# One image per half pass: another order of all steps in a fused transformer tower on one core

## The chip, the cores and the metric

The kernel runs on one core of a Trainium2 chip. Time is the device time of one launch in microseconds (us), all 64 images, loading of weights and storing of results included. Engines are named by what they do: TensorE (PE, products; PEld is its loading of weights), VectorE (DVE), ScalarE (ACT), GpSimd (POOL), SyncE (SP, here the one that issues DMAs). Each has a queue of its own and takes it strictly in order; between engines there are only semaphores.

## The reference

For 64 images of 3x224x224:

```python
h = tok(x)                                   # 16x16 patches: layernorm, 768->192, layernorm, class token
h = h + attn(layernorm(h))                   # 12 heads of 64; q and k scaled by their norm over the heads
h = h + ffn(layernorm(h))                    # attention 2: 12 heads of 16, qkv with a gated LoRA delta (8 experts, top 2)

# attn
q, k, v = split(x @ w_qkv.T)                 # 3 x 768
q = q * rsqrt(norm(q, over heads) + eps);  k likewise
out = softmax(q @ k.T / scale[h]) @ v;  return out @ w_out.T + b_out
# ffn
probs = softmax(x @ Wg.T + bg);  combine = top 2 of probs
delta = ((x A + ba) * combine) @ Bm + combine @ bb
qkv = x @ Wqkv.T + bqkv + 2 * delta
return softmax(q @ k.T / 4) @ v @ Wproj.T + bproj
```

197 tokens an image, width 192, all float32.

## The kernel before

The work of one image is cut into named steps. Each step is a piece for several engines: TensorE makes products into banks of PSUM, ScalarE or VectorE read them, later steps use what they wrote. The steps, in the order in which an image passes them:

- X (ScalarE squares of the patches into qk_sq, GpSimd sums them), EMB (embedding product), LA, LB, LC (layernorms on VectorE, GpSimd gives 1/sqrt), T1 (transpose of the hidden state; ScalarE copies it rounded to 16 bit, VectorE the remainder).
- Attention 1: QK.0 to QK.2 (queries and keys; ScalarE squares them into qk_sq and copies them), S (VectorE adds the squares), PS (product that adds pairs; ScalarE makes 1/sqrt of the norm in four passes), N.0 to N.3 (N.0, N.2: VectorE scales; N.1, N.3: ScalarE writes the high half qh or kh, VectorE the low half), V.0 and V.1 (values), SM.0 to SM.5 (scores of two heads each from the high halves; VectorE takes each row's maximum, after SM.5 it negates them), NT (transpose of the maxima; ScalarE copies them to neg_t), ST.0 to ST.5 (exact scores, transposed, minus the maximum; ScalarE takes the exponential into one of four ebufs), PV.0 to PV.2 (four heads each: row sums first, of which ScalarE makes the reciprocal, then the product with the values), M.0 to M.2 (VectorE multiplies with the reciprocal), OP (output projection, and VectorE adds), LD (layernorm), T2 (transpose).
- Attention 2: G and GB (gates), T3, QK2.0, QK2.1, V2, SM2.0 to SM2.2 (four heads each), NT2, ST2.0 to ST2.2, PV2.0 to PV2.2, M2.0 to M2.2, OP2, and the stores.

ORDER (line 51) is the order in which every engine issues its part of the steps, written out by hand. One run through it is a half pass: it begins one new image. A sign ahead of a step says whose: "+" the next image's, none this image's, "-" the previous one's, "=" the one before that. The number behind "@" is the first PSUM bank of the step. `half_pass` (line 62) reads it for the images of either parity; two half passes make one turn of the loop, and there are 32 turns, with half passes ahead of them and behind them in which only a part of the steps has an image. QK, V, SM, ST and PV take two banks, SM2 and ST2 four, all others one.

A step waits on TensorE until its banks have been read by whoever used them last (`users`, `reader`), and for its inputs. The waits are worked out from the order: `Pass.count` and `Pass.previous` find how often a semaphore has been raised when a given step of this or of the turn before is done, `wait` (line 342) emits the wait. So a new order moves the work and the waits and changes no instruction. Buffers that several steps share by turns: qk_sq (X and QK; freed by X's sums and by S), qh, ql, kh, kl (one set; N writes them, SM and ST read them), four ebufs (ST and ST2 in turn), two rinv.

The shapes of the products, as rows x columns of the array: T1, T2, T3, NT, NT2, QK, QK2, PS, EMB, V, V2, OP, OP2 and G use the whole array (98 to 128 rows); SM and ST 64 rows; SM2 and ST2 32 rows; PV and PV2 32 columns.

Of the kernel before, what the change touches and what calls it, by code (L numbers as in the profile page):

```python
# [27 lines left out]
NT = NP + 1  # L28
# [20 lines left out]


ORDER = """
+X T1@4 =QK2.0@1 =QK2.1@0 QK.0@2 =SM2.0@4 QK.1@0 QK.2@2 =SM2.1@4 -ST.3@0 -ST.4@4 -ST.5@2 -PV.1@6 S
-M.1 =SM2.2@0 -PV.2@4 PS@1 =NT2@7 -M.2 N.0 N.1 N.2 +EMB@2 -OP@3 N.3 =ST2.0@4 V.0@0 SM.0@2 =ST2.1@4
-LD =V2@0 SM.1@4 SM.2@2 -T2@6 =PV2.0@7 SM.3@4 =M2.0 =ST2.2@0 =PV2.1@6 SM.4@4 SM.5@0 -G@7 =PV2.2@2
NT@4 V.1@0 ST.0@4 =M2.1 ST.1@6 +LA =M2.2 -GB +LB ST.2@2 =OP2@5 -T3@4 +LC PV.0@6 M.0
"""


# [17 lines left out]
POS = {p: n for n, p in enumerate(SCHED)}  # L76
# [9 lines left out]
def banks(p):  # L86

    return range(BANK[p], BANK[p] + (4 if p[0] in QUAD else 2 if p[0] in WIDE else 1))


def head2(u, j):

    return 2 * j + u if u < 2 else 8 + j
# [60 lines left out]
def vit_tower(nc, x_t, w_emb, ln1, ln1_bias, tok_const, tok_bias, w_qk, w_v, w_out, w_gl, w_qkv2, w_lora_b,  # L154
# [4 lines left out]
    with ctx:  # L159
# [182 lines left out]
        def wait(eng, now, sig, p, earlier=None, by=1):  # L342


            n = now.count(steps[sig[0]], p, earlier)
            if n is not None:
                eng.wait_ge(sig[1], n * by)

        def reader(p, bank=None):

            if p[0] in QUAD and bank is not None and bank < BANK[p] + 2:
                return rd_lo[p[0]], p
            return rd_sig[p[0]], ({"PV": "M", "PV2": "M2"}.get(p[0], p[0]), *p[1:])

        def wait_free(eng, now, order, freed):


            q, earlier = now.previous(order, now.at)
            wait(eng, now, *freed(q), earlier)

        def passes(eng, body):
            body(Pass("start", -1))
# [15 lines left out]
        for j in range(4):  # L378
            loads.append((sel2_raw[32 * j:32 * j + 32], head_rows[64:96, 0:G2]))
            for u in range(2):  # L380
                g, r = divmod(head2(u, j), 4)
# [15 lines left out]
        for part in range(3):  # L397
            r = slice(64 + GPITCH * part, 64 + GPITCH * part + NE + 1)
# [129 lines left out]
        def _(pe):  # L528
# [38 lines left out]
            def body(now):  # L567
                for p in now.steps():
# [12 lines left out]
                            pe.wait_ge(setup_dve, 5)  # L581

                    freed = [(b, *now.previous(users[b], p)) for b in banks(p)]
                    for sig, q, earlier in dict.fromkeys((*reader(q, b), earlier) for b, q, earlier in freed):
                        wait(pe, now, sig, q, earlier)
                    if kind == "EMB":
                        pe.wait_ge(x_loaded[s], (now.image(p) + 1) * 16)
# [38 lines left out]
                    elif kind == "SM":  # L626
                        wait(pe, now, high_N, ("N", s, 3))
                        for t in range(2):
                            for e in range(2):
                                r = slice(64 * e, 64 * e + 64)  # L630
# [3 lines left out]
                    elif kind == "SM2":  # L634
                        wait(pe, now, high_QK2, ("QK2", s, 1))
                        for t in range(2):
                            for j in range(4):
                                r = slice(32 * j, 32 * j + 32)
# [7 lines left out]
                    elif kind == "ST":  # L646
                        wait(pe, now, qkn_ready, ("N", s, 3))
                        wait(pe, now, rd_sig["NT"], ("NT", s, 0))
                        for t in range(2):
# [3 lines left out]
                            for n, (left, right) in enumerate(terms):  # L653
                                for e in range(2):
                                    r = slice(64 * e, 64 * e + 64)
                                    nc.tensor.matmul(ps(p, slice(0, TR), slice(NT * t, NT * t + NT), e),  # L656
                                                     left[r], right[r], start=(n == 0), stop=False)
                            for e in range(2):
                                r = slice(64 * e, 64 * e + 64)
# [3 lines left out]
                    elif kind == "ST2":  # L663
                        wait(pe, now, rd_sig["QK2"], ("QK2", s, 1))
                        wait(pe, now, rd_sig["NT2"], ("NT2", s, 0))
                        for t in range(2):
# [4 lines left out]
                            for n, (left, right) in enumerate(terms):  # L671
                                for j in range(4):
                                    r = slice(32 * j, 32 * j + 32)
# [80 lines left out]
                    mm.then_inc(pe_sig[kind][1], 1)  # L754

            passes(pe, body)

        @block.scalar
        def _(act):
# [11 lines left out]
            def body(now):  # L771
                act.sem_clear(act_chain)
                count[0] = 0
                for p in now.steps():
# [3 lines left out]
                    if kind == "X":  # L778
# [3 lines left out]
                        if not first:  # L782
                            wait_free(act, now, sq_users, squares_used)
                            if now.image(p) == 0:
                                act.wait_ge(setup_dve, 2)
# [11 lines left out]
                    elif kind == "QK":  # L797
                        wait(act, now, pe_sig[kind], p)
                        src = psum[:, b:b + 2, 0:2 * NT]
                        if i == 0:  # L800
                            wait_free(act, now, sq_users, squares_used)
# [43 lines left out]
                    elif kind in ("ST", "ST2"):  # L845
                        wait(act, now, pe_sig[kind], p)
                        for half in range(2 if kind == "ST2" else 1):
                            n = e_order.index((p, half)) % EBUFS
                            wait_free(act, now, e_users[n], exp_used)
                            nc.scalar.activation(  # L850
                                ebuf[n].rearrange("p e a t -> p e (a t)"),
                                psum[0:TR, b + 2 * half:b + 2 * half + 2, 0:2 * NT], ACT.Exp
                            ).then_inc(rd_lo[kind][1] if kind == "ST2" and half == 0 else done, 1)
# [450 lines left out]
```

## Time and profile before

| | us |
|---|---|
| median of the runs (3) | 3115.53 |
| lowest, highest | 3112.74, 3116.41 |
| the profiled execution, its own time | 3115.51 |
| its span in the trace | 3113.7 |
| TensorE busy | 2965.3 (95%) |
| VectorE busy | 2328.8 (75%) |
| ScalarE busy | 1963.5 (63%) |
| GpSimd busy | 591.9 (19%) |

A busy matmul row is not the array at its peak: matmuls overlap, and their ends are modelled. Starts are recorded; so the length of a step on TensorE is read as the distance from its first start to the first start of the next step. The views print a group of like instructions with its start, the time it covers and, in brackets, the idle time before it and what ended it.

### The profile page before, as it was taken

The page shows a single profiled execution, that of the slowest core. Times are in us where ns is not written, and L with a number is a line of the kernel's source. Part 1 is how long each engine was busy: PE and PEld are TensorE (multiplying, and loading weights), DVE is VectorE, ACT ScalarE, POOL GpSimd, SP SyncE. Part 2 cuts the span into 40 slices and gives each one's busy share as a digit, 9 for nine tenths or more (in the row PEclk, how much of TensorE's full clock was granted, in tenths as well). Part 3 has the DMA queues.
Part 4 walks back from the last instruction along what each step waited for, and adds up shares of the span by engine and source line. Part 5 has one row for each costly group of instructions (what it writes and reads, how often), then busy time and mean ns, then how long its engine had stood idle before and what let it go on. Part 6 is the DMA issues. An engine that isn't in the chain of part 4 may idle for free.

```text
span 3113.7 us, 98361 instructions
## 1 busy us (share of the span) xinstructions
PE 2965.3 (95%) x41624; PEld 2430.5 (78%) x41624; DVE 2328.8 (75%) x5441; ACT 1963.5 (63%) x3777; POOL 591.9 (19%) x859
## 2 busy tenths in 40 slices
PE   4899999999999999999999999999999999999996
PEld 4778877877877877877877888778778778778775
DVE  5777777777777777787777777777777777777773
ACT  2566666666666666666666666666666666666663
POOL 2111121121121121121121121121111111111210
PEclk7999999999999999999999999999999999999998
DMA  4000000000000000000000000000000000000000
GB/s 116 9 22 12 22 22 12 21 22 12 21 22 12 22 22 12 22 21 12 22 21 12 22 22 12 22 17 16 22 14 19 22 12 21 22 12 22 14 4 7
DMA packets 28389, 61.28 MB, mean 20 GB/s; under 512 B 4210, under 2 KB 18389, under 8 KB 27958
## 3 DMA queue, kind: packets, MB, share of 16 engines
q1 hardware_dynamic: 27958, 54.98, 6.1%
q8 instruction: 337, 5.52, 0.8%
q14 instruction: 94, 0.77, 0.1%
HBM read 45.29 MB, written 9.68 MB: 18 GB/s over the span
## 4 chain that ended last, share of the span: by engine, by line
PE 59%; DVE 35%; ACT 3%; issue 3%; DMA 0%; SPq 0%; POOL 0%; DVEq 0%; ACTq 0%
PE psum L686 9%; DVE mx L1118 8%; PE psum L695 8%; PE psum L590 8%; PE psum L612 7%; PE psum L622 4%; PE psum L722 4%; PE psum L674 3%; PE psum L656 3%; DVE st L1009 3%; DVE mx L1131 2%; PE psum L725 2%; DVE qk L1210 2%; PE psum L732 2%; DVE late L1227 2%
## 5 line engine op out<-in xcount | busy, mean ns | idle before, releaser
L850 ACT ACTIVATE ebufs<-psum 99x788 f32<-99x788 f32 x768 | 592.0, 823 | 58.1 <-PE psum L674 45.1
L519 POOL TENSOR_TENSOR veps<-mv,eps_ln 99x2 f32<-99x2 f32 x256 | 116.1, 453 | 2274.1 <-DVE mv L1040 1352.3
L1131 DVE TENSOR_REDUCE mx<-psum 99x4 f32<-99x788 f32 x384 | 357.5, 974 | 137.7 <-PE psum L639 137.4
L1118 DVE TENSOR_REDUCE mx<-psum 99x4 f32<-99x788 f32 x384 | 362.9, 974 | 52.1 <-PE psum L631 52.1
L612 PE MATMUL psum<-hn_s,qk_w 128*128 128x197 f16 x3840 | 354.9, 249 | 14.2 <-DVE hn_s L1082 7.2
L612 PEld LDWEIGHTS psum<-hn_s,qk_w 128*128 128x128 f16 x3840 | 323.0, 98 | 34.9 <-DVE qk L1210 19.0
L686 PE MATMUL psum<-ebufs,vx 98*32 98x197 f32 (+1 forms) x6144 | 293.6, 330 | 0.0
L695 PE MATMUL psum<-out_w,qk 128*99 128x192 f32 x1536 | 263.8, 329 | 0.1
L590 PE MATMUL psum<-emb_w,xb 128*99 128x193 f32 x1536 | 263.9, 327 | 0.0
L590 PEld LDWEIGHTS psum<-emb_w,xb 128*99 128x99 f32 x1536 | 249.1, 166 | 1.8 <-issue 1.4
L686 PEld LDWEIGHTS psum<-ebufs,vx 98*32 98x32 f32 (+1 forms) x6144 | 201.2, 110 | 57.5
L695 PEld LDWEIGHTS psum<-out_w,qk 128*99 128x99 f32 x1536 | 245.1, 166 | 0.3 <-issue 0.3
L622 PE MATMUL psum<-v_w,hn_s 128*99 128x384 f16 x1280 | 234.1, 330 | 0.0
L656 PE MATMUL psum<-qh,kh 64*99 64x197 f16 x1536 | 208.5, 255 | 17.5 <-DVE mx L1131 17.0
L1101 DVE TENSOR_TENSOR qk<-qk,ss 128x1182 f32<-128x1182 f32 x64 | 89.0, 1391 | 168.0 <-ACT ss L826 168.0
L802 ACT ACTIVATE qk_sq<-psum 128x788 f32<-128x788 f32 x192 | 158.8, 827 | 70.6 <-PE psum L612 70.6
L656 PE MATMUL psum<-ql,kh 64*99 64x197 f16 x1536 | 202.1, 246 | 0.0
L660 PE MATMUL psum<-neg_t,head_sel 64*99 64x197 f16 x1536 | 201.9, 246 | 0.0
L656 PE MATMUL psum<-qh,kl 64*99 64x197 f16 x1536 | 201.8, 245 | 0.0
L622 PEld LDWEIGHTS psum<-v_w,hn_s 128*99 128x99 f16 x1280 | 155.0, 127 | 47.1
L831 ACT CAST kh<-qk 128x1182 f16<-128x1182 f32 x64 | 75.6, 1181 | 176.4 <-DVE qk L1106 176.4
L1148 DVE TENSOR_TENSOR qk<-psum,rinv 128x394 f32<-128x394 f32 x192 | 108.9, 567 | 102.8 <-ACT rinv L861 62.1
(172 smaller groups left out, 6444.3 us busy)
## 6 DMA issues: line engine op xcount, KB each, us to landing
xb<-x_t SPq DMA_DIRECT2D x64, 591.0 KB, 3.9
out<-h SPq DMA_DIRECT2D x128, 73.5 KB
out<-h SPq DMA_DIRECT2D x64, 0.8 KB
vx<-w_qk SPq DMA_DIRECT2D x2, 384.0 KB, 11.2
qk_sq<-w_emb SPq DMA_DIRECT2D x1, 576.0 KB, 3.7
vx<-w_qk SPq DMA_DIRECT2D x1, 576.0 KB, 8.3
out_w<-w_out SPq DMA_DIRECT2D x8, 72.0 KB
late<-w_lora_b SPq DMA_DIRECT2D x1, 480.0 KB
```

Of the source, the lines that this page charges most:

```text
L590: nc.tensor.matmul(ps(p, slice(0, TR), slice(194 * t, 194 * t + D + 1)), xb[s][:, c, tile_cols(t)], emb_w[:, c, :], start=(c == 0), stop=( ...
L612: mm = nc.tensor.matmul(ps(p, slice(0, 128), slice(at, at + NT), m // 2), qk_w[:, w, f:f + 128], hn_s[s][:, v, c, 0:NT], start=(n == 0), s ...
L622: mm = nc.tensor.matmul(ps(p, slice(0, TR), slice(0, INNER // 2), b), hn_s[s][:, v, c, tile_cols(i)], v_w[:, w, INNER // 2 * b:INNER // 2 ...
L656: nc.tensor.matmul(ps(p, slice(0, TR), slice(NT * t, NT * t + NT), e), left[r], right[r], start=(n == 0), stop=False)
L660: mm = nc.tensor.matmul(ps(p, slice(0, TR), slice(NT * t, NT * t + NT), e), head_sel[r, 2 * i + e, :], neg_t[s][r, 0:NT], start=False, sto ...
L686: mm = nc.tensor.matmul(ps(p, slice(32 * j, 32 * j + 32), slice(NT * (c % 2), NT * (c % 2) + NT), c // 2), left, eb[0:n, j % 2, t, :], sta ...
L695: mm = nc.tensor.matmul(ps(p, slice(0, TR), slice(D * t, D * t + D)), o_t[s][:, m, tile_cols(t)], out_w[:, m, :], start=(m == 0), stop=(m ...
L722: nc.tensor.matmul(o, qkv2_w[:, w, f], hn2_s[s][:, v, c, 0:NT], start=(n == 0), stop=False)
L802: nc.scalar.activation(qk_sq[:, 4 * i:4 * i + 4, :].rearrange("p (b m) t -> p b (m t)", b=2), src, ACT.Square, scale=1 / WS)
L850: nc.scalar.activation(ebuf[n].rearrange("p e a t -> p e (a t)"), psum[0:TR, b + 2 * half:b + 2 * half + 2, 0:2 * NT], ACT.Exp).then_inc(r ...
L1118: nc.vector.tensor_reduce(mx[s][:, :, 2 * i:2 * i + 2].rearrange("p a e -> p e a"), psum[0:TR, b:b + 2, 0:2 * NT].rearrange("p e (a t) -> ...
L1131: nc.vector.tensor_reduce(mx2[s][:, :, at:at + 2].rearrange("p a e -> p e a"), psum[0:TR, b + 2 * half:b + 2 * half + 2, 0:2 * NT].rearran ...
```

## The change

All of ORDER is written anew: the order of the steps, their signs and their banks. Seen from an image, SM.2 to SM.5, NT, ST.0 to ST.2, PV.0 and M.0 come in the half pass after the one in which they came before ("-" instead of none); SM.0 and SM.1 stay in it, at its end. T3 goes from "-" to "=", T1 from none to "+" (from the start of a half pass to the end of the one before). The other steps keep their sign and change places and banks. SM stands in pairs, ST.2 to ST.5 in one run, PV.1 beside PV.2 and PV2.1 beside PV2.2.

The second part lets a wait be worked out where the step that used a bank or a buffer is of the turn before, but the step that frees it of this turn: `release` says "earlier" only where the freeing step is at or behind the user in the order.

```diff
 ORDER = """
-+X T1@4 =QK2.0@1 =QK2.1@0 QK.0@2 =SM2.0@4 QK.1@0 QK.2@2 =SM2.1@4 -ST.3@0 -ST.4@4 -ST.5@2 -PV.1@6 S
--M.1 =SM2.2@0 -PV.2@4 PS@1 =NT2@7 -M.2 N.0 N.1 N.2 +EMB@2 -OP@3 N.3 =ST2.0@4 V.0@0 SM.0@2 =ST2.1@4
--LD =V2@0 SM.1@4 SM.2@2 -T2@6 =PV2.0@7 SM.3@4 =M2.0 =ST2.2@0 =PV2.1@6 SM.4@4 SM.5@0 -G@7 =PV2.2@2
-NT@4 V.1@0 ST.0@4 =M2.1 ST.1@6 +LA =M2.2 -GB +LB ST.2@2 =OP2@5 -T3@4 +LC PV.0@6 M.0
++X =T3@3 QK.0@4 QK.1@6 -SM.2@2 -SM.3@0 QK.2@4 -SM.4@6 -SM.5@2 =QK2.0@1 S =QK2.1@6 =V2@4 =SM2.0@0
++EMB@7 -NT@5 =SM2.1@0 -ST.0@4 -ST.1@6 PS@0 =SM2.2@4 -PV.0@2 -M.0 N.0 -ST.2@4 -ST.3@0 +LA -ST.4@2
+-ST.5@6 =NT2@1 N.1 -PV.1@4 -M.1 -PV.2@6 -M.2 N.2 =ST2.0@0 N.3 -OP@4 =ST2.1@0 V.0@6 -LD =PV2.0@3 +LB
+=M2.0 =ST2.2@4 -T2@2 V.1@0 =PV2.1@5 +LC =PV2.2@3 =M2.1 -G@2 =M2.2 -GB +T1@4 SM.0@0 SM.1@6 =OP2@2
 """
...
+        def release(q, freed, earlier):
+
+            sig, r = freed
+            assert earlier or POS[r] >= POS[q]
+            return sig, r, earlier and POS[r] >= POS[q]
+
         def wait_free(eng, now, order, freed):
-
-
             q, earlier = now.previous(order, now.at)
-            wait(eng, now, *freed(q), earlier)
+            wait(eng, now, *release(q, freed(q), earlier))
...
-                    for sig, q, earlier in dict.fromkeys((*reader(q, b), earlier) for b, q, earlier in freed):
+                    for sig, q, earlier in dict.fromkeys(release(q, reader(q, b), earlier) for b, q, earlier in freed):
```

## Rows read from the trace of the kernel before

**Rows 1.** The page: the span, busy times, and the granted clock in 40 slices.

```profile
span 3113.7 us, 98361 instructions
PE 2965.3 (95%) x41624; PEld 2430.5 (78%) x41624; DVE 2328.8 (75%) x5441; ACT 1963.5 (63%) x3777; POOL 591.9 (19%) x859
...
PEclk7999999999999999999999999999999999999998
```

**Rows 2.** Windows: stretch, its length, busy time of each engine (instructions), clock, DMA.

```profile
1453.60:1500.60 47.00, 45.88 (x654) 37.60 (x658) 35.95 (x85) 30.64 (x60) 9.12 (x13) 1.00 0.06 18
1500.60:1547.60 47.00, 45.88 (x654) 37.66 (x658) 35.95 (x85) 30.63 (x60) 9.12 (x13) 1.00 0.06 18
```

**Rows 3.** The chain of waits from 1519 to 1536: start, length, piece.

```profile
1519.92 1.61 DVE mx L1118 x2
...
1534.78 0.58 DVE hn L1018 x2
...
1535.50 0.63 PE psum L563 x4
```

**Rows 4.** TensorE's timeline of one period: start, time covered, line, operands.

```profile
1500.53 0.88 PE L686 MATMUL psum<-ebufs,ones_col 98*32 98x197 f32 x16
...
1521.29 0.37 PE L631 MATMUL psum<-kh,qh 64*99 64x197 f16 x4
1522.00 0.46 PE L674 MATMUL psum<-qk 32*99 32x197 f16 x12 [0.34 <-issue]
...
1523.63 0.88 PE L631 MATMUL psum<-kh,qh 64*99 64x197 f16 x8
1524.44 1.17 PE L705 MATMUL psum<-gl_w,ss 128*99 128x136 f32 x8
...
1535.50 0.63 PE L563 MATMUL psum<-mats_sb,hn 98*128 98x98 f32 x4 [0.26 <-DVE hn L1018]
...
1540.51 0.38 PE L639 MATMUL psum<-qk 32*99 32x197 f16 x8
1540.99 3.64 PE L612 MATMUL psum<-hn_s,qk_w 128*128 128x197 f16 x40
...
1546.03 0.29 PE L656 MATMUL psum<-qh,kh 64*99 64x197 f16 x2 [0.28 <-DVE mx L1131]
...
1547.53 0.88 PE L686 MATMUL psum<-ebufs,ones_col 98*32 98x197 f32 x16
```

**Rows 5.** The same timeline: one SM step and then ST2, two SM steps and then T2.

```profile
1516.93 0.38 PE L631 MATMUL psum<-kh,qh 64*99 64x197 f16 x4
1517.24 0.46 PE L674 MATMUL psum<-qk 32*99 32x197 f16 x12
...
1519.51 0.55 PE L631 MATMUL psum<-kh,qh 64*99 64x197 f16 x8
1519.99 0.57 PE L563 MATMUL psum<-mats_sb,hn 98*128 98x98 f32 x4
```

**Rows 6.** Groups by line and shape: count, busy us, mean ns of one, idle before.

```profile
L850 ACT ACTIVATE ebufs<-psum 99x788 f32<-99x788 f32 x768 | 592.0, 823 | 58.1 <-PE psum L674 45.1 <-PE psum L660 7.0
L1118 DVE TENSOR_REDUCE mx<-psum 99x4 f32<-99x788 f32 x384 | 362.9, 974 | 52.1 <-PE psum L631 52.1
...
L501 POOL TENSOR_TENSOR qk_sq<-qk_sq 128x591 f32<-128x591 f32 x63 | 91.2, 1448 | 65.5 <-ACT qk_sq L786 65.5
```

**Rows 7.** Timelines of the start (VectorE, TensorE) and of the end (TensorE).

```profile
80.19 0.17 DVE L975 MEMSET gl_w<- 64x136 f32 x1
...
92.40 1.39 DVE L1093 TENSOR_TENSOR qk_sq<-qk_sq 128x1182 f32<-128x1182 f32 x1
125.05 0.63 PE L563 MATMUL psum<-mats_sb,hn 98*128 98x98 f32 x4 [0.71 <-DVE hn L1018]
...
3079.74 0.59 PE L722 MATMUL psum<-hn_s,qkv_w 128*128 128x197 f16 x5 [1.61 <-DVE late L1200]
...
3106.30 4.13 PE L751 MATMUL psum<-proj_w,late 128*99 128x192 f32 x12 [1.78 <-DVE late L1227]
```

## The prediction

> **What bounds the kernel now.** The page first: TensorE is busy 95% of the span, at full granted clock in every slice but the first and last [rows 1]. So ask for the period. One half pass is one image; the busy times of two neighbouring windows of 47.00 us repeat to 0.01 us [rows 2], so the loop is steady: 47.00 us an image, TensorE 45.88 busy, VectorE 35.95, ScalarE 30.6. The chain of waits then says who holds TensorE: for 15.6 us of each period (1519.92 to 1535.50) it lies on VectorE, from SM.2's maximum to LC, and ends where T1 (L563) waits for LC's hn [rows 3]. TensorE is nearly level with it there, so the loss must be read from TensorE's own timeline: the start of a step against the start of the next, compared with the pitch where nothing waits [rows 4]. Lost are 0.41 us before ST2.2 (0.71 for an SM step that takes 0.31 elsewhere), 0.33 at T1, 0.26 between SM.4 and SM.5 (0.81 for two, 0.48 elsewhere), 0.40 before ST.4 (maxima of SM2.1), 0.17 between SM2.0 and QK.1; with three of 0.05 to 0.07, 1.8 us. What stays, 45.2 us, is TensorE's own work, about 96% of the period. An order alone can win at most the 1.8 and what changes of product shape cost.
>
> **Fewer changes of shape.** I write the steps of one half pass in a row and mark the tile of the array: whole (T, QK, EMB, V, OP, G, NT, PS), half height (SM, ST), quarter height (SM2, ST2), quarter width (PV, PV2). Before there are 27 changes in a period, after it 25: SM in three pairs instead of 1, 2, 1, 2; PV.1 beside PV.2, PV2.1 beside PV2.2; the whole-tile runs are one more. One SM step alone takes 0.31 us to the next step's start, two take 0.48, not 0.62 [rows 5]: joining saves 0.14. I take 0.13 for each of the three joins (one of SM, two of PV), and 0.1 back for the added whole-tile run: 0.3 us a period. Bounds: nothing, and 0.6 (TensorE's rows with the steps' new neighbours). No instruction is added or removed, so the floor is 45.2 less 0.3: 44.9 us. Against it stands the sum over the steps in their new order, each from its start to the next one's where nothing waits (one period of TensorE's timeline, 47 groups of lines; its first and last in [rows 4], others in [rows 5]): T3 0.35, QK.0 1.71, QK.1 and QK.2 1.79 each, SM pairs 0.48 (three), QK2 2.74, V2 1.45, SM2 0.31 (three), EMB 4.22, NT and NT2 0.27, ST 0.68 a step and 0.13 a run (6, two runs), PS 0.70, PV 2.15 and 4.17 for the pair, ST2 0.82 (three), OP 4.05, V 1.76 (two), PV2 0.81 and 1.48 for the pair, T2 0.41, G 1.01, T1 0.55, OP2 2.03: 44.7 us. I go on with 44.7, the nearer to the single steps, and add each wait found on the way.
>
> In a pair an SM step takes 0.24 us of TensorE [rows 5], its maximum on VectorE 0.97 from start to end [rows 6], 0.9 from one start to the next. The Trainium skill, TensorEngine Tiling (Array Packing), PSUM Bottleneck, states this as a rule that speaks against the change: tiling speeds up the products and not the reading of PSUM; the trace agrees, and rival C works out what it would do here.
>
> **Moved waits.** I lay TensorE's steps end to end from T3 (0) and carry VectorE's and ScalarE's queues in program order beside them, with the durations of [rows 6]; those without a row are the start-to-start distances of the engines' timelines in the same period, which sum to the 35.95 and 30.6 of [rows 2].
> *T3 to SM2.1.* VectorE ends GB at -0.2, then T1 0.5, SM.0 and SM.1 1.8: ends 2.15. QK.1@6 needs SM.1's bank and could start at 2.06: waits 0.15. Then OP2 0.5, T3 0.7, SM.2 and SM.3 from 4.4, SM.4 and SM.5 to 8.6, QK2.0 to 9.2, S (1.4 for its first add [rows 7], 1.2 for two smaller ones) to 11.8, QK2.1 to 12.85, SM2.0 to 14.6. SM2.1 reaches banks 0 to 3 at 15.7, behind EMB's 4.2 us: margin 1.1. EMB and NT, which cover the VectorE queue, are why the crowd of maxima costs nothing; without them SM2.1 would wait 3.4 us.
> *ScalarE and GpSimd.* X's squares (ScalarE 1.17, then GpSimd 1.45+0.55+0.53) share qk_sq with QK.0. X comes behind T1 and the gates: starts at -1.6, GpSimd is ready at 2.3. QK.0's ScalarE part (0.83+4x0.32=2.0) ends at 4.35; QK.2@4 needs it and comes at 4.48. QK.1's ends at 6.1, SM.4@6 comes at 6.27. Margins of 0.15: no wait, but tight.
> *NT to PV.* ST.0 waits for neg_t (copy ends 16.15): 0.14. SM2.2@4 waits for ST.1's exponentials (0.73, done 18.55): 0.2. PS's four passes (2.35) hold back PV.0's reciprocal to 21.6, M.0 ends 22.15; ST.4@2 comes at 22.45: no wait. ST.0 to ST.2 and PV.0 are only moved; their exponentials now stand at 0.73 us against 0.69 us of TensorE, which runs ahead under PV.1 and PV.2.
> *N.* N.1 writes qh behind ST.5's exponentials: 25.1 to 26.2 on ScalarE, its low part on VectorE to 27.5, M.1 28.0, M.2 (PV.2 ends 28.3) 28.95: OP at 29.2 is free. N.3 ends at 33.2, nobody waits.
> *OP to T3.* OP's VectorE part ends 34.7, GpSimd's rstd 35.75, LD 36.4, T2 comes at 37.6. ST2.2@6 waits for V.0's copy: 0.13. LB 37.0 to 39.4 and LC at 41.55 stand before T1 (42.25): the old wait of T1 is gone, margin 0.3. G's maxima 43.15, M2.2 43.45: OP2 waits 0.22. GB ends 45.35, T3 comes at 45.5.
> Sum of the new waits 0.84: 44.7+0.84 = 45.5 us a period, 1.5 less than 47.00. Old waits all go: T1 now has LC well ahead; ST2.2 follows PV2.0 instead of SM.3; SM.4/SM.5 and ST.5 have banks that are long free. What is late next is VectorE's GB (0.15) and the ring through X (0.15).
> For a wait I may have missed I take up to 0.9 (half of the old sum); for waits that overlap, -0.35: period 45.15 to 46.4.
>
> **Start.** Before, T1 of half pass 2 starts at 125.05 [rows 7]; 30 periods before the T1 of 1535.50 is 125.5, so it is steady from there on. After T1 of image 1 VectorE prepares attention 2's weights, 80.19 to 92.40: 12.2 us [rows 7]. After the change image 1 has no SM.2 to SM.5, NT, ST of image 0 ahead: T1 at about 67, weights until 81, SM.0 and SM.1 until 82.7, and only then QK.1 (bank 6): a new wait of some 12 us, half pass 1's zero at 80.6. Without the "=" steps it takes about 38 (33 of TensorE and two gaps at NT/ST.4 and T2): half pass 2 at 118.5, 6.5 sooner. Bounds: 112 (the weights fall beside work) and 127 (all 12 us beside nothing).
> **End.** Half pass 64 begins 32 periods behind 1535.50, at 3039.5; before, the last two so take 3113.7-3039.5 = 74.2. After, number 64 has all of SM.2 to PV.2: TensorE 30 us, with waits for the maxima (4x0.9), T2 and GB 39. Number 65 is attention 2 alone: before, QK2 at 3079.74 to OP2 at 3106.30, OP2 4.1 (twice its 2.03 in the loop, so at the lower level of 1.2 GHz; the page's last slice grants 0.8 on average [rows 1]) and 3.3 for its addition and store [rows 7]; T3 and the bank waits of SM2.1, ST2.1 are the same: 33. Together 72; bounds 68 and 78.
>
> **Sum.** 118.5 + 62x45.5 + 72 = 3011.5 of span; the profiled execution has 3115.51 for 3113.7, so +1.8: 3013.3, that is 3013. Its own time is the median of the runs shown (3115.53), so no more is added. From 45.15 and 46.4: 2992 and 3069, and with the edges' bounds all on one side 2982 and 3084.
>
> **Rivals.**
> A, my forecast, 45.15 to 46.0 a period, 2992 to 3044: chance 0.60. Below 45.15 (waits that overlap): 0.06.
> B, only the joins pay: the 1.8 us of waits go from their old places and come back in others of the same size (many steps now wait for one bank: ST.4, V.1, OP2). 47.00-0.3 = 46.7: 118.5+62x46.7+72+1.8 = 3088. For it: VectorE works as long as before and the old order was tight in the same way; against it: in my table it idles at five places, 9.5 us, spread out. Chance, with all between 46.0 and 47.05: 0.20.
> C, slower: maxima crowd VectorE between T1 and SM2.1 (13.3 us of work in 15.7). Its queue is strict, so SM.4, SM.5 wait for the ScalarE of QK.1, this for QK.0, this for GpSimd's squares of X, and S, QK2.1 and SM2.0 stand behind. It costs nothing until the queue is 1.1 us late, from there one for one; slower from 2.75 us late, a period of 47.15; at 3.0 late 45.5+1.9 = 47.4: 118.5+62x47.4+72+1.8 = 3131. For it: margins of 0.15 in a row; against: GpSimd's 2.5 us are the same in every period of before, and each link would have to slip by half a microsecond. Chance 0.09.
> D, no net change (47.05 to 47.25, 3109 to 3122): 0.05.
>
> **How the numbers follow.** Time 3013, the likeliest case. The range is 2988 to 3090: below it 0.03, above it C, D and the top of B, 0.17; it holds B's own 3088. What is told apart from no change here is 0.2%, 6 us. Faster by more: A, its lower tail and B: 0.86; within: D, 0.05; slower: C, 0.09.
>
> **What would show it.** Right: windows of 45.5 us that repeat; no idle before L563 for L1018; PE idle at L612 (QK.1) for L1118, at L631 none inside a pair, at L639 for L850; the chain mostly on TensorE. In the start one TensorE idle of about 12 us that ends with L1118 near 82.7. Wrong: a period above 46.4; a chain through L501/L502/L503 and L802, or SM2.1 (L639) waiting for L1131: then C's queue is the bound; SM pairs that still take 0.6 us: then joins pay nothing.

## The result: 1.6% slower, and the profile after

After the change the kernel takes 3166.40 us (median of 4 runs, 3165.43 to 3167.41) against 3114.71 (4 runs, 3112.74 to 3116.41): ratio 1.0163, 95% interval 1.0151 to 1.0175. The forecast was 3013, and the sign was wrong too; the time lies beyond those of all four rivals as well, C's 3131 included. The profiled execution took 3167.41, its span 3165.6. Line numbers behind the order's lines are those of before plus 4; in some experiments the same operation stands a line or two further down still.

The page says little at first sight. TensorE is 26 us less busy than before, VectorE 141 us more, though no instruction was added (5441 on VectorE before and after [rows 1]).

```profile
span 3165.6 us, 98297 instructions
PE 2939.4 (93%) x41624; PEld 2432.9 (77%) x41624; DVE 2470.0 (78%) x5441; ACT 1955.1 (62%) x3777; POOL 531.4 (17%) x859
...
PEclk7899999999999999999999999999999999999997
```

Two windows of one period each, cut inside T3, 0.37 us behind its first start (columns as in [rows 2]):

```profile
1512.80:1560.47 47.67, 45.48 (x652) 37.82 (x650) 38.23 (x85) 30.48 (x59) 8.14 (x14) 1.00 0.06 18
1560.47:1608.14 47.67, 45.47 (x652) 37.59 (x650) 38.23 (x85) 30.50 (x59) 8.13 (x14) 1.00 0.06 18
```

The loop is steady again, at 47.67 us instead of 47.00. The same 85 VectorE instructions cover 38.23 us where they covered 35.95. Some of them have become longer. The groups by line and shape say which (busy us, mean ns of one). After:

```profile
L1197 DVE TENSOR_TENSOR gl<-gl,comb 99x256 f32<-99x256 f32 x64 | 103.5, 1617 | 2.2
L1067 DVE SCALAR_TENSOR_TENSOR h<-lnt,mv,tokc 99x192 f32<-99x192 f32 x128 | 80.4, 666 | 1.1 <-POOL rstd L526 1.1
L523 POOL TENSOR_TENSOR veps<-mv,eps_ln 99x2 f32<-99x2 f32 x256 | 50.8, 198 | 2310.1 <-DVE mv L1016 1310.7 <-DVE mv L1044 999.4
```

and before:

```profile
L1193 DVE TENSOR_TENSOR gl<-gl,comb 99x256 f32<-99x256 f32 x64 | 27.2, 425 | 2.2
L1063 DVE SCALAR_TENSOR_TENSOR h<-lnt,mv,tokc 99x192 f32<-99x192 f32 x128 | 47.4, 412 | 2.2 <-POOL rstd L522 2.2
L519 POOL TENSOR_TENSOR veps<-mv,eps_ln 99x2 f32<-99x2 f32 x256 | 116.1, 453 | 2274.1 <-DVE mv L1040 1352.3 <-DVE mv L1012 921.8
```

GB's last product (gl times comb) takes 1617 ns instead of 425, LB's first operation 666 instead of 412 (there are two of it in a period). These two make 1.70 of the 2.28 us that VectorE is busy longer; no other group grew by more than 0.04 us a period, and the rest is that neighbouring operations overlap less. GpSimd's small sum at the layernorms takes 198 ns instead of 453. Put the timelines of VectorE, GpSimd and TensorE in one period beside each other, in this order:

```profile
1510.62 1.67 DVE L1197 TENSOR_TENSOR gl<-gl,comb 99x256 f32<-99x256 f32 x1
1512.21 0.56 DVE L1086 TENSOR_TENSOR hn_s<-psum,hn_s 128x394 f16<-128x394 f32 x1
```

```profile
1502.10 1.00 POOL L517 TENSOR_TENSOR h<-h,rowc 99x384 f32<-99x384 f32 x1 [0.79 <-DVE hn L1022]
...
1510.56 1.44 POOL L505 TENSOR_TENSOR qk_sq<-qk_sq 128x591 f32<-128x591 f32 x1 [2.36 <-ACT qk_sq L790]
1512.08 0.59 POOL L506 TENSOR_TENSOR qk_sq<-qk_sq 128x197 f32<-128x197 f32 x1
```

```profile
1502.28 0.46 PE L678 MATMUL psum<-qk 32*99 32x197 f16 x12 [0.25 <-issue]
...
1509.19 2.16 PE L755 MATMUL psum<-proj_w,late 128*99 128x192 f32 x12 [0.49 <-DVE late L1231]
1512.43 0.36 PE L556 MATMUL psum<-mats_sb,gl 98*128 98x98 f32 x2 [1.08 <-DVE gl L1197]
...
1516.42 0.55 PE L635 MATMUL psum<-kh,qh 64*99 64x197 f16 x8
1516.96 1.28 PE L616 MATMUL psum<-hn_s,qk_w 128*128 128x197 f16 x13
```

GpSimd's first sum of X's squares starts at 1510.56 and ends at 1512.00. VectorE's product is issued at 1510.62, 0.06 us behind it, and ends at 1512.29: most of its own work comes only once the sum is over. T3 (L556) waits for it. The new order puts X first in the half pass, directly behind GB, so the two meet in every period. The same instruction, in the half passes at the end in which no image is begun and GpSimd has nothing to sum, is short:

```profile
3083.67 0.42 DVE L1197 TENSOR_TENSOR gl<-gl,comb 99x256 f32<-99x256 f32 x1
```

TensorE's losses in the period, by the distance of a step's last start from the next step's first, less the distance without a wait (about 0.09 to 0.26 us by shape): T3 1.24, OP2 0.56, SM2.2 0.38, ST2.2 0.32, ST.0 0.27, three small ones 0.27: 3.04 us. What is left, 44.63, is TensorE's own work.

The whole against the forecast, in the span: the first T3 starts at 127.30 (forecast 118.5, +8.8); 62 periods to the T3 at 3084.25 are 47.69 on average (forecast 45.5, +135.9); the rest is 81.4 (forecast 72, +9.4). Together +154.1, which is 3165.6 less the 3011.5 of the sum.

### The profile page after: what moved, and what is told of

The parts are those of the page before. It is cut to its first block, busy times and chain, and to the rows that moved or that the text cites. A ratio compares the mean times of both kernels' runs of the same rounds, so it can differ in the third digit from the quotient of the medians.

```text
span 3165.6 us, 98297 instructions
## 1 busy us (share of the span) xinstructions
PE 2939.4 (93%) x41624; PEld 2432.9 (77%) x41624; DVE 2470.0 (78%) x5441; ACT 1955.1 (62%) x3777; POOL 531.4 (17%) x859
## 4 chain that ended last, share of the span: by engine, by line
PE 82%; DVE 10%; issue 4%; ACT 3%; DMA 0%; SPq 0%; POOL 0%; DVEq 0%; ACTq 0%
PE psum L690 13%; PE psum L616 11%; PE psum L699 8%; PE psum L594 8%; PE psum L626 7%; PE psum L660 6%; PE psum L678 5%; PE psum L748 5%; PE psum L726 4%; DVE gl L1197 3%; PE psum L709 2%; PE psum L729 2%; PE psum L635 2%; PE psum L556 2%; ACT ebufs L854 2%
## 5 line engine op out<-in xcount | busy, mean ns | idle before, releaser
L523 POOL TENSOR_TENSOR veps<-mv,eps_ln 99x2 f32<-99x2 f32 x256 | 50.8, 198 | 2310.1 <-DVE mv L1016 1310.7
L660 PE MATMUL psum<-qh,kh 64*99 64x197 f16 x1536 | 201.6, 251 | 12.6 <-ACT neg_t L845 12.6
L845 ACT CAST neg_t<-psum 128x197 f16<-128x197 f32 x64 | 20.9, 326 | 274.5 <-PE psum L556 274.2
L526 POOL TENSOR_TENSOR rstd<-veps,half_neg 99x2 f32<-99x2 f32 x256 | 179.0, 699 | 20.1
L678 PE MATMUL psum<-qk 32*99 32x197 f16 x4608 | 156.0, 251 | 18.0 <-issue 15.8
```

The lines of the kernel that those rows point to most:

```text
L526: nc.gpsimd.tensor_tensor(rstd[part][s][:], veps[part][s][:], half_neg[:], ALU.pow).then_inc(rstd_ready[1], 1)
L678: mm = nc.tensor.matmul(ps(p, slice(0, TR), slice(NT * t, NT * t + NT), j), left[r], right[r], start=(n == 0), stop=(n == 3))
```

## Experiments

The local memory is SBUF, in which all buffers lie but the banks of PSUM. Theory P (in the expectations also "port"): while a GpSimd instruction that reads the local memory runs, a VectorE operation with two inputs there is held until it ends. Rival Q: the VectorE work is slow, or TensorE late, for reasons of the new order itself, and the stall at T3 only shows them.

### The sums held until GB's product is done

```diff
 if p[0] == "X":
     wait(pool, now, xsq_ready, p)
+    wait(pool, now, hw_ready, ("GB", 1 - s, 0))
```

> The kernel after, with one more wait: GpSimd begins the sums of X's squares only when VectorE has ended GB of the image before. Theory P (port): after's loss in front of T3 comes from GB's last product (L1197, two inputs in SBUF, 1.67 us instead of 0.43), which is held while GpSimd runs its first sum (L505). Then L1197 is 0.43 again, TensorE's wait in front of T3 falls from 1.24 to at most 0.2, the period from 47.67 to 46.4 to 46.6 us and the time from 3166 to about 3095 (3085 to 3105), faster than before. Rival Q (queue): VectorE's queue from G to GB is too long by itself for the place of T3; L1197 may change, but T3 still waits about 1 us, period 47.4 or more, 3150 or more (the later sums may even add).

3114.30 us, ratio to before 0.9995 (0.9986 to 1.0004): 52 us less than the order as it was given, all of its loss against the kernel before, by one wait on an engine that is 17% busy. It missed the 3085 to 3105 of theory P. GB's product is short again in every half pass. The period is 46.78.

```profile
L1198 DVE TENSOR_TENSOR gl<-gl,comb 99x256 f32<-99x256 f32 x64 | 27.2, 425 | 2.2
```

Less came than expected, because a wait took part of its place: QK.0's squares use X's buffer, the sums are now later, and QK.2 waits for the ScalarE part of QK.0.

```profile
1536.31 0.55 PE L636 MATMUL psum<-kh,qh 64*99 64x197 f16 x8
1537.22 1.88 PE L617 MATMUL psum<-hn_s,qk_w 128*128 128x197 f16 x20 [0.36 <-ACT qk L811]
```

By starts, SM.3's last to QK.2's first, this wait is 0.43 us. It is the ring through X of which the forecast had said that it had 0.15 us to spare.

### A third of the sum

GpSimd's first sum runs over 197 columns instead of 591. Two thirds of the first sum are left out.

```diff
-link(nc.gpsimd.tensor_tensor(sq[:, 0:3, :], sq[:, 0:3, :], sq[:, 3:6, :], ALU.add))
+link(nc.gpsimd.tensor_tensor(sq[:, 0:1, :], sq[:, 0:1, :], sq[:, 3:4, :], ALU.add))
```

> The kernel after, with GpSimd's first sum over 197 instead of 591 columns (two thirds of it are left out of the computation). It begins where it did, ahead of L1197 by 0.06 us, and lasts about 0.55 instead of 1.44. Theory P: L1197 ends about 0.3 us behind the end of that sum, so it lasts 0.8 to 0.9 us; T3 comes 0.8 earlier, period 46.8 to 47.0, time about 3120. If the second sum takes its turn first, L1197 lasts 1.4 and the period is 47.4. Rival (a slowdown by shared bandwidth and not by exclusion): L1197 runs slower only while the sum runs, so about 0.43 to 0.7 long. Rival Q: T3 waits as before, 3160.

3112.86 us (one run), period 46.82. The product follows the length of the sum beside it:

```profile
L1197 DVE TENSOR_TENSOR gl<-gl,comb 99x256 f32<-99x256 f32 x64 | 52.0, 812 | 2.2
...
L505 POOL TENSOR_TENSOR qk_sq<-qk_sq 128x197 f32<-128x197 f32 x63 | 38.5, 610 | 145.1 <-ACT qk_sq L790 145.1
```

The sum is 0.84 us shorter and the product 0.81. If the two shared a path, each at part of its speed, the sum would have been stretched as well; it takes its usual time (1453 ns after, 1448 before [rows 6]).

### The other collision: GpSimd's add at LD

LB's first operation (0.67 instead of 0.41 us) lies beside GpSimd's add of the bias at LD (L517 at 1502.10 above). Here the add is issued at G.

```diff
-elif p[0] == "LD":
-    wait(pool, now, hn2_ready, p)
+elif p[0] == "G":
+    wait(pool, now, hn2_ready, ("LD", s, 0))
```

> The kernel after, with GpSimd's addition of b_proj (L517, 1.0 us) issued at step G instead of at LD, so it no longer lies beside LB's first product (L1067, 1.27 us for two against 0.74 elsewhere). Theory P: L1067 is back to 0.74 for two. LB has a margin in front of T1, so the period stays within 0.1 of 47.67: 3160 to 3170. Rival: LB's half microsecond is carried through LC and G's queue to T3: period 47.15, 3134.

3190.91 us, ratio 1.0238 (1.0223 to 1.0254): worse than after. LB's operation is back at 409 ns, as expected. But the add now holds another operation, which has 16 columns and stands ahead of M2.2 on VectorE. OP2 waits for M2.2 (VectorE, GpSimd and TensorE of one period):

```profile
1614.14 0.17 DVE L1174 TENSOR_REDUCE gmax<-gl 99x2 f32<-99x16 f32 x1
1614.34 0.59 DVE L1175 TENSOR_TENSOR gl<-gl,gmax 99x16 f32<-99x16 f32 x1
1614.86 0.35 DVE L1231 TENSOR_TENSOR late<-psum,late 128x197 f32<-128x197 f32 x1
```

```profile
1613.90 1.00 POOL L517 TENSOR_TENSOR h<-h,rowc 99x384 f32<-99x384 f32 x1
```

```profile
1615.36 2.16 PE L755 MATMUL psum<-proj_w,late 128*99 128x192 f32 x12 [0.91 <-DVE late L1231]
```

The whole period is longer by 0.40 (48.07), the 0.42 by which OP2 is later; GB's collision stays behind it. The reduction at 1614.14 runs inside the add (1613.90 to 1614.90) in its usual 0.17 us: it has one input. What the short LB operation gives back is worth nothing here. In after, VectorE's part of T2 (L1086) follows at 1505.56 without idle time; here it waits for ScalarE:

```profile
1611.31 0.57 DVE L1086 TENSOR_TENSOR hn_s<-psum,hn_s 128x394 f16<-128x394 f32 x1 [0.47 <-ACT hn_s L800]
```

From there on to G's first operation the two kernels are the same to 0.01 us, and in both VectorE stands idle for 0.16 us ahead of it and waits for TensorE's G. The expectation named LB alone; what the moved instruction meets in its new place had not been looked up, the same mistake as in the prediction.

### T3 out of the way instead of the sum

```diff
-+X =T3@3 QK.0@4 QK.1@6 ...
++X QK.0@4 =T3@3 QK.1@6 ...
-... -G@2 =M2.2 -GB +T1@4 SM.0@0 ...
+... -G@2 =M2.2 +T1@4 -GB SM.0@0 ...
```

> The kernel after, with two swaps in the order: T1 ahead of GB, T3 behind QK.0. Nothing is done about the collision, T3 only gets 1.7 us more of TensorE's work ahead of it. If the wait at T3 is one of length alone (both P and Q say so), it vanishes, whether L1197 takes 1.67 or 0.43: period 46.4 to 46.7, 3090 to 3105. Against it: QK.0 now needs T1's remainder 0.3 to 0.5 us earlier, and its squares wait for GpSimd's sums, since QK.0 comes 1.2 us earlier while X doesn't: then 0.3 to 0.8 us of idle at QK.2 or SM.4, period 47.0 to 47.3, 3130 to 3145.

3205.12 us, ratio 1.0283 (1.0266 to 1.0300), period 48.29. above both expected figures (46.4 to 46.7 and 47.0 to 47.3). By starts, T3 waits only 0.12 us. But GB still meets the sum, one operation earlier, and the maxima behind it on VectorE are late, for which QK.1's bank waits: 1.21 us. SM.2 waits 0.49 more for T3's bank, which is now written, and so read, later.

```profile
1624.07 1.04 DVE L1190 TENSOR_TENSOR rest<-gates,rest 99x16 f32<-99x16 f32 x1
1625.14 0.21 DVE L1192 TENSOR_TENSOR comb<-rest,gsum 99x48 f32<-99x48 f32 x1
1625.38 0.64 DVE L1197 TENSOR_TENSOR gl<-gl,comb 99x256 f32<-99x256 f32 x1
```

```profile
1623.61 1.46 POOL L505 TENSOR_TENSOR qk_sq<-qk_sq 128x591 f32<-128x591 f32 x1 [2.36 <-ACT qk_sq L790]
1625.15 0.59 POOL L506 TENSOR_TENSOR qk_sq<-qk_sq 128x197 f32<-128x197 f32 x1
```

L1190 has 16 columns and takes 0.17 us elsewhere. Here (VectorE above, GpSimd below) it ends at 1625.11, 0.04 behind the sum. The next with two inputs meets the second sum. So what a held operation loses is set by what is left of GpSimd's instruction, not by its own size.

### The collision alone, put into the kernel before

```diff
+spare_a, spare_b = sb("spare_a", [128, 3, NT]), sb("spare_b", [128, 3, NT])
 ...
+elif p[0] == "GB":
+    wait(pool, now, gexp_ready, ("G", s, 0))
+    nc.gpsimd.tensor_tensor(spare_a[:], spare_a[:], spare_b[:], ALU.add)
```

> The kernel before with one more GpSimd instruction a half pass: a sum of 128x591 on two spare buffers of its own, issued when the gates' exponentials are there (step GB). Nothing reads it and the order stays the old one. Theory P (while a GpSimd sum of SBUF operands runs, VectorE's operations with two SBUF inputs are held until it ends, tiny ones too): one of GB's small operations or its product stretches from below 0.5 us to 1.0 to 1.6 us, LB, LC and T1 are later by 1.0 to 1.3; T1 already waited 0.33, so the period goes from 47.00 to 47.9 to 48.2, time 3170 to 3190. Rival Q (the long product after the change comes from its new place beside other VectorE or PSUM work, not from GpSimd): the added sum changes nothing on VectorE, period 47.00, time 3115.

3181.30 us, ratio 1.0212 (1.0196 to 1.0227), period 48.08: what theory P gave, and 66 us for an instruction that nobody waits for. VectorE, GpSimd and TensorE of one period:

```profile
1565.47 1.24 DVE L1191 TENSOR_TENSOR rest<-gates,rest 99x16 f32<-99x16 f32 x1
```

```profile
1565.23 1.45 POOL L514 TENSOR_TENSOR spare_a<-spare_a,spare_b 128x591 f32<-128x591 f32 x1
```

```profile
1571.72 0.63 PE L568 MATMUL psum<-mats_sb,hn 98*128 98x98 f32 x4 [1.32 <-DVE hn L1023]
```

T1 waited 0.26 by this column [rows 4] and waits 1.32 now. The old order, old places and old buffers rule out Q as far as the held operation goes. (The diff above doesn't show the lines that fill the two spare buffers with zeros at the start.)

### X elsewhere in the order

```diff
-+X =T3@3 QK.0@4 ... =V2@4 =SM2.0@0
+=T3@3 QK.0@4 ... =V2@4 +X =SM2.0@0
```

> The kernel after with one step moved in the order: X (ScalarE's squares of the next image's patches and GpSimd's three sums) from the front of the half pass to a place behind V2, ahead of SM2.0. The sums no longer meet GB, LB or SM.0. Theory P: GB's product 0.43 us instead of 1.62, T3 no longer waits (1.24 to about 0.1), period 47.67 - 1.1 = 46.4 to 46.9 (EMB's last products may wait up to 0.5 us for the sums), time 3090 to 3118. Rival Q (the lost time of this order comes from the queue of maxima; removing one stall brings out another of like size): period above 47.3, time over 3140.

3148.89 us, ratio 1.0109 (1.0094 to 1.0124), period 47.31: the time is outside P's figures (46.4 to 46.9, 3090 to 3118) and just inside Q's (above 47.3, over 3140). The mechanism is not the one that Q named, the queue of maxima. P's first half holds: GB's product is 425 ns and T3 doesn't wait. But the sums now end too late for EMB's last products, and NT, ST.0 and SM2.2 stand behind them.

```profile
1619.44 0.51 PE L604 MATMUL psum<-emb_w,xss 128*99 128x1 f32 x4 [0.64 <-POOL xss L507]
```

By starts this wait is about 0.8 us; I had taken 0.5 at most. The start is 7 us longer as well, its first T3 at 134.5; EMB's last products wait 3.44 us for the sums there too.

### The same with NT ahead of EMB

```diff
-+EMB@7 -NT@5 =SM2.1@0 ...
+-NT@5 +EMB@7 =SM2.1@0 ...
```

> The last kernel with NT ahead of EMB instead of behind it, so that the copy of the negated maxima to neg_t lies beside EMB's products, and the sums of X have 0.3 us more before EMB's last products. Theory P with the waits read from the trace after (ST.0 0.27): ST.0's wait goes, period 46.2 to 46.5, time 3075 to 3095: faster than before. Rival (NT waits for the last maxima, SM.5's, and for their negation on VectorE behind SM2.0's maximum): NT comes too soon and gains nothing or loses up to 0.3 us, period 46.5 to 47.0, time 3095 to 3125.

3140.33 us, ratio 1.0080 (1.0065 to 1.0095), period 47.19. Both expected figures (46.2 to 46.5 and 46.5 to 47.0) were too low. EMB's last products still wait 0.66 us by starts for the sums, where the kernel above had 0.81. ST.0's wait goes, and ST.1 right behind it has one instead (0.37). Its second bank is 7, EMB's, which VectorE has to read first, and NT no longer stands between the two.

```profile
1566.24 0.29 PE L660 MATMUL psum<-qh,kh 64*99 64x197 f16 x2
...
1567.34 0.29 PE L660 MATMUL psum<-qh,kh 64*99 64x197 f16 x2 [0.21 <-issue]
```

### The start: attention 2's weights later

The second image's first steps, after (TensorE):

```profile
67.56 0.89 PE L567 MATMUL psum<-mats_sb,hn 98*128 98x98 f32 x4 [11.00 <-DVE hn L1022]
...
85.06 3.29 PE L616 MATMUL psum<-hn_s,qk_w 128*128 128x197 f16 x20 [11.88 <-DVE mx L1122]
...
127.30 0.56 PE L556 MATMUL psum<-mats_sb,gl 98*128 98x98 f32 x2 [3.71 <-DVE gl L1197]
```

The wait of 11.88 at QK.1 was forecast as "some 12", until 82.7; it ends at 85.06. In the experiment VectorE prepares the weights behind SM.1's maxima of image 0 and not ahead of them.

```diff
 # VectorE's T1, second image
-    weights_of_attention2()
 ...
 # VectorE's SM
+if i == 1 and s == 0 and now.image(p) == 0:
+    weights_of_attention2()
```

> The kernel after with the preparation of attention 2's weights (13 us on VectorE, once) called at VectorE's SM.1 of image 0 in the second image's pass instead of at T1, so that T1's remainder and the first maxima don't stand behind it. Theory (the start lost 9.2 us against the forecast mostly because TensorE stands 11.9 us at QK.1 behind this work): the wait of 11.9 shrinks to 6 to 9, the first T3 comes at 122 to 125 instead of 127.7, the period stays 47.67, time 3161 to 3164. Rival (VectorE is needed as a whole there, so the same work is paid wherever it stands): first T3 within 1 us of 127.7, time 3165 to 3167.

3161.01 us, ratio 1.0147 (1.0130 to 1.0164), 5.4 below after. The period is untouched (47.67).

```profile
83.51 0.57 PE L635 MATMUL psum<-kh,qh 64*99 64x197 f16 x4 [6.23 <-DVE mx L1120]
...
123.22 0.56 PE L556 MATMUL psum<-mats_sb,gl 98*128 98x98 f32 x2 [3.72 <-DVE gl L1197]
```

### X's squares in a buffer of their own

The first experiment, and the buffer that QK.2's wait hangs on made separate.

```diff
-xsq = qk_sq[:, 0:KC, :]
+xsq = sb("xsq", [128, KC, NT])[:]
 ...
-sq_users = [p for p in SCHED if p[0] == "X" or p[0] == "QK" and p[2] == 0]
+x_users = [p for p in SCHED if p[0] == "X"]
+sq_users = [p for p in SCHED if p[0] == "QK" and p[2] == 0]
 ...
     if kind == "X":
-        wait_free(act, now, sq_users, squares_used)
+        wait_free(act, now, x_users, squares_used)
```

> The kernel after with GpSimd's sums of X held until GB's product is done (as in the first experiment) and X's squares in a buffer of their own instead of in qk_sq, so that QK.0's squares don't wait for the later sums. Theory P (what this order still pays for GpSimd is the exclusion at GB, and once the sums are out of its way only the shared buffer): QK.2's wait of 0.43 us goes, period 46.78 - 0.43 = 46.35 (46.25 to 46.45), time 3085 to 3092, faster than before. Rival (the queue of maxima is full there: QK.2 or SM.4 then waits for VectorE instead): period 46.6 to 46.8, time 3103 to 3115.

3090.76 us, ratio 0.9915 (0.9898 to 0.9931), period 46.42. QK.2 follows SM.3 without a wait:

```profile
1526.79 0.55 PE L637 MATMUL psum<-kh,qh 64*99 64x197 f16 x8
1527.33 1.88 PE L618 MATMUL psum<-hn_s,qk_w 128*128 128x197 f16 x20
```

### Both together

> The last kernel with the preparation of attention 2's weights called at SM.1 of the second image's pass. Theory: the start gains what it gained alone (first T3 4.1 us sooner, half pass 64 0.9 shorter), the period stays that of the last kernel, time 5 us below it, 3080 to 3087 and 0.990 of before. Rival (with the shorter period the start no longer hangs on VectorE): within 2 us of the last kernel.

3085.77 us, ratio 0.9901 (0.9886 to 0.9916), faster than both kernels: period 46.42, first T3 at 121.95, half pass 64 at 43.59 instead of 44.48. The new order is 1% faster than the kernel before once the collision at GB and the shared buffer are gone and the weights are moved. Whether the old order would gain by the same three edits was not tried, so this 1% is not the worth of the order alone.

## Why the prediction was wrong

**The step that failed** is the sentence "GB ends 45.35, T3 comes at 45.5". It took GB's operations at their durations of before, in a place where GpSimd's 1.45 us sum starts beside them. The sum's start was in my own table ("X comes behind T1 and the gates: starts at -1.6", ScalarE 1.17, then GpSimd: -0.4), and GB's end too (-0.2), so the two overlapped there. I checked GpSimd only as a link of a chain (who waits for its result), not as a neighbour. Apart from the hold the margin of 0.15 was about right: the product would have ended at 1511.04 and T3 come at 1511.2. The error is 1.24 us of wait in 62 periods, 77 of the 154 us; taking it away alone gave 52, since 0.43 came back at QK.2.

The evidence was in the trace of before. L519 has 256 instances of mean 453 ns, of which only one in four is long: 1.25 us at 1516.43, beside VectorE's kl (L1113, 1516.27 to 1517.63), against 0.20 at 1514.38 (kernel before, GpSimd and then VectorE):

```profile
1514.38 0.20 POOL L519 TENSOR_TENSOR veps<-mv,eps_ln 99x2 f32<-99x2 f32 x1 [21.23 <-DVE mv L1040]
...
1516.43 1.25 POOL L519 TENSOR_TENSOR veps<-mv,eps_ln 99x2 f32<-99x2 f32 x1 [1.08 <-DVE mv L1012]
```

```profile
1516.27 1.36 DVE L1113 TENSOR_TENSOR kl<-qk,kh 128x1182 f16<-128x1182 f32 x1
```

A group whose mean is more than twice its usual duration should have made me ask what stood beside it.

The Trainium skill says it in SBUF — State Buffer, section SBUF: two separate sides: GpSimd and VectorE have one pair of ports in common, which is locked and not divided; whichever of the two starts first keeps it for its whole instruction. On VectorE's side this concerns a fast mode and, where GpSimd's instruction reads that memory, operations with two inputs there. The traces agree: 1617 ns against 425, 1.04 us against 0.17, a product that shrinks by 0.81 when the sum shrinks by 0.84. I didn't weigh it. Even so the forecast's own table would not have settled it: it has the product start at -0.62 (0.42 ahead of GB's end) and the sum at -0.43, so that the product goes first and loses nothing. On the chip the sum is ahead by 0.05 to 0.06 us in all 61 half passes in which the two meet. A table that is 0.2 us off could give either order, 45.5 or, with the wait of 1.24, 46.7; the second should have stood as a rival.

**The other waits.** Forecast 0.84 together; measured 1.80 without T3's. OP2 0.56 (forecast 0.22: M2.2 stands behind three of G's operations), SM2.2 0.38 (0.20), ST2.2 0.32 (0.13), ST.0 0.27 (0.14), QK.1 none (0.15), three of 0.07 to 0.10 that I had not listed (0.27). Of the five steps that I named four did wait, at about twice the size (1.53 against 0.69). My reading, not tested, is that in a table where queues meet exactly all errors go to one side, since a queue that is early gains nothing. That is 0.96 a period, a second term of the sum that was too small, and it stays when the collision is gone: 46.42 against 45.5. So the forecast of 45.15 to 46.0 would have failed without the collision too.

**What was right.** The floor: 44.63 against 44.7, so the joins pay (two SM steps take 0.54 us, from 1516.42 to QK.2 at 1516.96, its small wait included, and none has idle time inside the pair). The old waits at T1, from SM.4 to SM.5 and at ST.4 went; ST2.2, which waited 0.41 before, still waits 0.32 in its new place. Rival C, crowded maxima, didn't happen: QK.1 doesn't wait, and SM2.1 has none of the long waits it would show. Rival B had the old 1.8 us of waits come back in other places: apart from T3's the trace has 1.80. With T3's wait and the shared buffer out of the way the kernel takes 3091 us, and B had said 3088. That the times agree so closely is in part luck: the period is 46.42 and not B's 46.7, and the longer start and end make up for it. What B lacked is the collision.

**Start and end.** The start is 8.8 us late. QK.1 comes 2.4 late. The weights take 13.4 us on VectorE instead of 12.2, and 1.0 of the difference is the same hold once more: two operations of one column, which take 0.46 us together before, stand beside the first sum of X (GpSimd, 70.14 to 71.59) and take 1.45 (VectorE, before and after):

```profile
80.76 0.46 DVE L978 TENSOR_TENSOR kmask<-mats_sb 128x1 f32<-128x1 f32 x2
```

```profile
70.23 1.45 DVE L982 TENSOR_TENSOR kmask<-mats_sb 128x1 f32<-128x1 f32 x2
```

Then there are waits of 1.90 at T1, 0.90 at EMB and 0.51 at ST.0 that I hadn't counted, and 3.71 at T3 with GB's collision again. Moving the weights gave 4.1 of it. The end is 9.4 late: half pass 64 took 44.5 (forecast 39), the last 36.9 (forecast 33). No experiment was aimed at it; the trace shows waits with no other work to lie beside (TensorE):

```profile
3087.21 0.72 PE L635 MATMUL psum<-kh,qh 64*99 64x197 f16 x12 [2.43 <-DVE h L1236]
3088.65 0.57 PE L635 MATMUL psum<-kh,qh 64*99 64x197 f16 x4 [0.73 <-DVE mx L1122]
...
3098.94 0.38 PE L643 MATMUL psum<-qk 32*99 32x197 f16 x8 [1.85 <-DVE mx L1135]
```

For the last one I had counted from QK2 and not from T3, which starts 2.1 us sooner, and the sum itself was wrong: from QK2 at 3079.74 to the end at 3113.7 are 34.0 us, not 33.

**Open** is which of the 0.96 could be ordered away; NT ahead of EMB only moved one wait. LB's hold beside the LD add (0.52 us of VectorE a period) is still there in the fastest kernel. By the trace of the deferred add its removal only lengthens VectorE's idle time ahead of G, and in the fastest kernel too VectorE waits for TensorE there (0.17); so it seems to cost nothing. No run took it away without putting another hold in its place.

## What to carry to other kernels

When work of GpSimd or VectorE is moved, lay the two engines' timelines over each other in the new order and look for a GpSimd instruction beside VectorE operations with two inputs in the local memory: the smallest of them can be held until it ends. Hold or shift the instruction of the idle engine, not the one on the path, look up what it meets there, and see which buffer is now freed later. Don't trust a table made by hand to 0.2 us: the waits of 0.13 to 0.22 that this one gave were 0.27 to 0.56 where they came at all, and it had the order of two starts the wrong way round.

## What the runs showed of the hardware

- A VectorE operation of 99x16 with two inputs in the local memory takes 0.17 us, and 1.04 to 1.24 when a GpSimd sum of 128x591 (1.45) is under way; it ends 0.03 to 0.04 us behind the sum. One of 99x256 (0.42 alone) ends 0.28 behind it. All GpSimd instructions here read the local memory, so no run tells whether one that only writes holds too.
- Not held were, beside GpSimd's instructions, a reduction with one input (0.17 at 1614.14, with the add deferred) and an operation with one input in PSUM (0.56 at 1512.21 in after, beside the second sum, 0.57 elsewhere).
- The hold goes both ways: GpSimd's 0.20 us instruction took 1.25 beside VectorE's kl.
